# TensorE takes half of a repetition's queries between the first tile's state and the second tile's keys

## The chip, the cores and the metric

The kernel runs on one core of a Trainium2 chip. The metric is the time of one execution on the device in microseconds (us). A core has TensorE (PE; its weight loads are listed apart as PEld), VectorE (DVE), ScalarE (ACT), GpSimd (POOL) and SyncE (SP, which here only issues DMAs). They run side by side and wait for each other on semaphores.

## The reference

One transformer layer over 4 sequences of 2048 tokens with 256 features. The first half is a linear attention with 16 heads of 16 features, the second a mixture of eight experts of which each token takes two:

```
q = relu(x Wq + bq);  k = relu(x Wk + bk);  v = x Wv + bv
q_ = [q*sin(place), q*cos(place)];  k_ = [k*sin(place), k*cos(place)]
kv = k_^T v                        (one state for each head of a sequence)
attn = (q_ kv) / max(q_ . sum(k_), 1e-4)
x = layernorm(x + attn Wo + bo)
gate = softmax of the 2 largest of x router_w^T
out = sum over the 2 experts e of gate_e * (gelu(x w1_e^T) w2_e^T)
x = layernorm(x + out)
```

The state of a sequence needs all of its 2048 tokens before the first of them can be attended to.

## The kernel before

The 8192 tokens are cut into 32 pairs of two tiles of 128 tokens. A repetition of the first stage (`rep`, 0 to 31) projects pair `i = rep` to keys, values and queries, and from repetition `LAG` = 9 on also attends pair `j = rep - 9`, which belongs to the sequence before. Repetitions 10 to 31 project the attention of pair j-1 out, and 11 to 31 also route pair j-2 to its experts. Then 135 expert steps follow, which also finish the attention of the last pairs. Products are made of three float32r passes (`PASSES`: high x high, high x low, low x high), so a product over 256 features is six matmuls.

The order of the work is written out by hand: each engine has its own function `step(u, rep)`, and waits on semaphores that the others raise. Repetitions 0 to 3, 8 to 11, 16 to 19, 24 to 27, 30 and 31 are straight code on TensorE, those between run as loops of two repetitions (`pipeline`). The numbers of the waits are then worked out in registers.

TensorE's order in a repetition from 9 on is: `keys_values` of tile 0 (L540, waits for the low part of x), `attend` of tile 0 (L577, waits for the query's low part L1185 and, from repetition 12 on, for L1171 of VectorE), `state` of the second tile of the pair before (L560), `keys_values` of tile 1 (its wait `k_ready` is for ACT's last read of the first tile's keys and values, L851), `attend` of tile 1, `project_out` of pair j-1 (L629, L631), `rank` (L641 to L645), `state` of tile 0 of this pair, `queries` of both halves (L613, twelve matmuls of 256 columns into the two halves of one PSUM bank), and `attention_transposed` (L600, four transposes). The last one waits for the division of the attention rows by their denominators (`at_ready`, L1058) and for `la_read`, the sum at L1091, in which VectorE reads the banks that `project_out` wrote and that the transposes write next.

```
                if rep > 0:
                    pe.wait_ge(q32_ready, i)
```

is how `queries` waits for ACT to have read the queries of the repetition before (the ReLU at L913). With its second half it raises `q_done`.

ACT's order: key ReLU, router part and the two scaled copies of the values for tile 0 (L847 to L851), cosine part of tile 0 (L831), high part of the next x (L823), the normalised rows of pair j-2 (L860; waits until earlier rows in the same buffer have been scattered), cosine part of tile 1 (L831), high part of a query (L877), an exponential (L881), keys and values of tile 1 (L847 to L851), the copy of the transposes (L869), the ReLU of the queries (L913, waits for `q_done`).

VectorE's order: sine part of tile 0 (L1047), after a whole sequence the state (L1068 on), the choice of experts (L1108 to L1125), sine part of tile 1 (L1047), the division (L1054 to L1058), the residual (L1150), the sum (L1091), the low part of a query (L1185), gates (L1132 to L1141), statistics (L1155, L1156), positions (L1171, L1175), means and logits, and the low part of the transposes (L1179). POOL makes the low part of x (L1576) and scatters the finished rows to the experts' regions in HBM (L1586): two scatters, then, behind the division of the current pair, two more.

Of the kernel before, what the change touches and what calls it, by code (L numbers as in the profile page):

```python
# [44 lines left out]
LAG = PB + 1  # L45
# [63 lines left out]
def build(nc, x, xT, WqT, bq, WkT, bk, WvT, bv, WoT, Wo, bo, bo_columns, rwT, w1T, w2T, consts, out):  # L109
# [4 lines left out]
    with ctx:  # L114
# [257 lines left out]
        def parts(rep):  # L372


            return (LAG <= rep, LAG < rep, LAG + 1 < rep, rep % PB == 0 and PB <= rep, PB <= rep)

        def lagged(u, rep):

            slot = (rep - LAG) % 2
            return u * 2 + (rep % 2 - LAG), u + (rep % 2 - LAG - slot) // 2  # L380
# [145 lines left out]
        def _(pe):  # L526
# [3 lines left out]
            def keys_values(i, rep, h):  # L530
                t = i * 2 + h
                if h == 0 and rep < XLO_POOL:
                    pe.wait_ge(xlo_ready, i + 1)
                elif h == 0:
                    pe.wait_ge(xlo_late, i - (XLO_POOL - 1))
                if rep > 0 or h > 0:
                    pe.wait_ge(k_ready, t)
                def product(n, bank, weights, columns):
                    k, (a, b) = n // len(PASSES), PASSES[n % len(PASSES)]
                    return nc.tensor.matmul(PS[:, bank, 0:columns], xs[:, rep % 2, a, k, h * P:(h + 1) * P], weights[:, b, k, :],  # L540
                                            start=(n == 0), stop=(n == 3 * KD - 1 and bank == bV), skip_group_check=True)

                for n in range(3 * KD):
                    product(n, bK, wk, KE)
                if rep == 0 and h == 0:
                    pe.wait_ge(bias_step, BIAS)
                nc.tensor.matmul(PS[:, bK, 0:D], ones_r[:], bias_k[:], start=False, stop=True, skip_group_check=True)  # L547
                for n in range(3 * KD):
                    mm = product(n, bV, wv, D)
                mm.then_inc(kv_done, 1)  # L550

            def state(t, rep_t):
                pe.wait_ge(k_ready, t + 1)
                pe.wait_ge(ones_ready, t + 1)
                if rep_t % NT_B == 0 and rep_t > 0:
                    pe.wait_ge(state_step, STATE * (rep_t // NT_B - 1) + STATE_READ)
                for half in range(KD):
                    for g in range(NQ):
                        rows_g = slice(g * QUAD, (g + 1) * QUAD)
                        mm = nc.tensor.matmul(PS[rows_g, bST, half * SW:(half + 1) * SW], kr[:, rep_t % 2, half, rows_g],  # L560
                                              vs[:, rep_t % 2, half, :, g, :],
                                              start=(rep_t % NT_B == 0 and half == 0), stop=(rep_t % NT_B == NT_B - 1),
                                              skip_group_check=True)
                mm.then_inc(st_done, 1)

            def attend(j, rep, h, ranked=None):
                if h == 0:
                    pe.wait_ge(qlo_ready, j + 1)
                    if ranked is not None:
                        pe.wait_ge(pos_step, ranked * POS + POS_READ)  # L570
                    if (rep - LAG) % PB == 0:
                        pe.wait_ge(state_step, STATE * ((rep - LAG) // PB + 1))
                if rep > LAG or h > 0:
                    pe.wait_ge(o_done, j * 2 + h)
                for half in range(KD):
                    for n, (a, b) in enumerate(PASSES):
                        mm = nc.tensor.matmul(PS[:, bN + half, 0:2 * NW], qs[:, a, half, h * P:(h + 1) * P],  # L577
                                              sts[:, b, half].rearrange("p a b -> p (a b)"),
                                              start=(n == 0), stop=(n == 2))
                mm.then_inc(n_done, 1)  # L580

            def router_products():
                pe.wait_ge(s_won, 16)
                pe.wait_ge(rw_step, 1)
                for m in range(KD):
                    for k in range(KD):
                        nc.tensor.matmul(PS[:, bA, m * E:(m + 1) * E], won[:, k, m * P:(m + 1) * P], rw[:, k, 0, :],
                                         start=(k == 0), stop=(k == KD - 1))
                for k in range(KD):
                    mm = nc.tensor.matmul(PS[:, bA, KD * E:(KD + 2) * E], ones_r[:].bitcast(F32),  # L590
                                          rw[:, k].rearrange("p a e -> p (a e)"), start=(k == 0), stop=(k == KD - 1))
                mm.then_inc(rw_done, 1)
# [11 lines left out]
            def queries(i, rep, halves):  # L604
                if rep > 0:
                    pe.wait_ge(q32_ready, i)
                if rep == 0:
                    pe.wait_ge(proj_low, 4)
                for half in halves:
                    n = 0  # L610
                    for k in range(KD):
                        for a, b in PASSES:
                            mm = nc.tensor.matmul(PS[:, bQ, half * PAIR:(half + 1) * PAIR],  # L613
                                                  wq[:, a, k, half * P:(half + 1) * P], xs[:, rep % 2, b, k, :],
                                                  start=(n == 0), stop=(n == 3 * KD - 1))
                            n += 1
                if KD - 1 in halves:
                    mm.then_inc(q_done, 1)

            def project_out(j, rep):  # L620
                pe.wait_ge(thi_ready, j + 1)
                if rep == LAG:
                    pe.wait_ge(proj_low, 6)
                    pe.wait_ge(bias_step, BIAS_OUT)
                for h, bank in ((1, bC), (0, bA)):
                    for n, (a, b, k) in enumerate(HIGH_FIRST):
                        if h == 1 and n == 2 * KD:
                            pe.wait_ge(tlo_ready, j + 1)
                        nc.tensor.matmul(PS[:, bank, 0:KE], aT[:, a, k, h * P:(h + 1) * P], wo[:, b, k, :],  # L629
                                         start=(n == 0), stop=False)  # L630
                    mm = nc.tensor.matmul(PS[:, bank, 0:KE], ones_r[:], bias_o[:], start=False, stop=True)  # L631
                mm.then_inc(w_done, 1)
# [15 lines left out]
            def step(u, rep):  # L648
                attn, onward, route, _, _ = parts(rep)
                i = u * 2 + rep % 2  # L650
                j = lagged(u, rep)[0]
                last = rep == NPAIR - 1
                if rep == LAG:
                    pe.wait_ge(dve_const, 2)
                    pe.wait_ge(pool_const, POOL_CONST)
                keys_values(i, rep, 0)
                if attn:
                    attend(j, rep, 0, j - 3 if rep > LAG + 2 else None)
                if 1 <= rep:
                    state(i * 2 - 1, 2 * rep - 1)  # L660
                if rep < LAG:
                    queries(i, rep, (0,))
                keys_values(i, rep, 1)
                if last:
                    queries(i, rep, (0, 1))
                if attn:
                    attend(j, rep, 1)
                if last:
                    pe.wait_ge(table_step, 1)
                if onward:  # L670
                    project_out(j - 1, rep - 1)
                if route:
                    rank(j - 2, rep - 1, j)
                state(i * 2, 2 * rep)
                if not last:
                    queries(i, rep, (1,) if rep < LAG else (0, 1))
                if rep == PRODUCTS_REP:
                    router_products()
                if last:
                    pe.wait_ge(k_ready, 2 * NPAIR)  # L680
                    table_turned(FIRST_MADE, bK)
                    state(i * 2 + 1, 2 * rep + 1)
                if attn:
                    attention_transposed(j, rep)
                if rep == NPAIR - 2:
                    counted(EARLY_PAIRS, EARLY_PAIRS + 1)
# [7 lines left out]
            def table_turned(n, bank):  # L694
                pe.wait_ge(table_step, n)
                nc.tensor.matmul(PS[0:2, bank, P:2 * P], table[:], ident, start=True, stop=True)\
                    .then_inc(tbl_done, 1)

            pipeline(pe, step)


# [70 lines left out]
            for s in range(STEPS):  # L772
# [20 lines left out]
                rep = None if j is None else LAG + j  # L793
# [965 lines left out]
```

## Time and profile before

| | us |
|---|---|
| median of 3 runs | 858.84 |
| lowest and highest of them | 858.13, 859.87 |
| the profiled execution | 858.07 |
| its span, first to last instruction | 856.3 |
| TensorE busy, of the span | 800.6 |
| VectorE busy | 566.9 |
| ACT busy | 460.2 |
| POOL busy | 428.8 |

Every number of the rows below comes from the one profiled execution, whose time is 1.8 us above its span. The first stage ends about 315 us into the span, the expert steps take the rest. A timeline row gives the start in us from the span's start, the duration in us, engine, line, operation, what is written and read, and how many instructions were merged; in brackets stands how long the engine was idle before, and what ended the wait. Matmuls overlap, so durations of neighbouring rows overlap too, and distances between starts are the safer measure.

### The profile page before, as it was taken

How to read it: one execution, taken by the hardware profiler on the slowest of the kernel's cores; microseconds unless marked ns; L12 is line 12 of the kernel's file. 1: busy time of each engine (PE TensorE's matmuls, PEld its weight loads, DVE VectorE, ACT ScalarE, POOL GpSimd, SP SyncE). 2: the span in 40 equal slices, each digit the busy share in tenths (PEclk: the TensorE clock that was granted, in tenths of full speed). 3: DMA queues.
4: the chain of work that ended last, by engine and by line, in shares of the span. 5: the costliest groups of instructions: out<-in, count | busy, mean ns of one | idle time of the engine just before them, and what ended most of it. 6: DMA issues, size and time to landing. Idle time of an engine off the chain costs nothing.

```text
span 856.3 us, 22053 instructions
## 1 busy us (share of the span) xinstructions
PE 800.6 (93%) x6684; PEld 736.7 (86%) x6684; DVE 566.9 (66%) x1816; ACT 460.2 (54%) x1044; POOL 428.8 (50%) x545
## 2 busy tenths in 40 slices
PE   5999999999899869999999999999999999999990
PEld 4888999889899858999899999989999999999980
DVE  3336788878888766666766666664444477777773
ACT  3556676666766644445444544434444445566653
POOL 3886566666677663444445444553222234444442
PEclk9999999999999978999999999999999999999996
DMA  6444033333333242332333332232322355666644
GB/s 195 164 139 133 26 115 121 101 102 107 105 101 101 89 154 82 101 96 89 90 102 106 101 98 85 88 107 82 120 76 78 122 186 191 223 224 215 227 168 172
DMA packets 56469, 106.64 MB, mean 125 GB/s; under 512 B 9262, under 2 KB 37552, under 8 KB 54449
## 3 DMA queue, kind: packets, MB, share of 16 engines
q1 hardware_dynamic: 41296, 63.25, 25.0%
q0 software_dynamic: 12624, 33.84, 10.8%
q10 hardware_dynamic: 2448, 8.26, 2.6%
q8 instruction: 58, 0.95, 0.5%
q14 instruction: 43, 0.34, 0.1%
HBM read 61.91 MB, written 44.32 MB: 124 GB/s over the span
## 4 chain that ended last, share of the span: by engine, by line
PE 80%; DVE 6%; issue 5%; ACT 5%; DMA 3%; SPq 1%; POOL 1%; ACTq 0%; POOLq 0%; DVEq 0%
PE PS L736 23%; PE PS L724 22%; PE PS L540 10%; PE PS L754 7%; PE PS L577 4%; PE PS L713 4%; PE PS L613 4%; PE PS L629 3%; PE PS L600 1%; PE PS L560 1%; ACT vs L851 1%; DMA boc<-in_bo_columns 1%; ACT vs L850 1%; PE PS L547 1%; DVE o L1047 1%
## 5 line engine op out<-in xcount | busy, mean ns | idle before, releaser
L1670 POOL DMA_INDIRECT token_rows<-xg x135 | 134.8, 998 | 284.0 <-DVE xg L1403 261.6
L736 PEld LDWEIGHTS PS<-w,hT 128*128 128x128 f32 x1620 | 211.7, 189 | 13.5 <-issue 3.7
L724 PE MATMUL PS<-w,xgT 128*128 x810 | 222.9, 411 | 0.0
L736 PE MATMUL PS<-w,hT 128*128 x1620 | 218.3, 284 | 0.8 <-ACT hT L994 0.8
L724 PEld LDWEIGHTS PS<-w,xgT 128*128 128x128 f32 x810 | 143.8, 191 | 24.3
L1586 POOL DMA_INDIRECT expert_rows<-rows,idx x128 | 131.0, 1024 | 60.1 <-issue 35.4
L994 ACT ACTIVATE hT<-PS 128x512 fp32r<-128x512 f32 x135 | 80.7, 598 | 142.1 <-PE PS L754 138.4
L990 ACT ACTIVATE hg<-PS 128x512 f32<-128x512 f32 x135 | 80.5, 596 | 118.4 <-PE PS L724 106.4
L1468 DVE TENSOR_TENSOR hT<-PS,hT 128x512 fp32r<-128x512 f32 x135 | 93.4, 692 | 75.6 <-ACT hT L994 75.6
L1395 DVE TENSOR_TENSOR xgT<-PS,xgT 128x256 fp32r<-128x256 f32 x135 | 57.0, 422 | 75.6 <-ACT xgT L960 57.6
L754 PE MATMUL PS<-cst,hg 128*128 128x128 f32 x540 | 81.5, 273 | 0.7 <-ACT hg L990 0.7
L540 PE MATMUL PS<-wk,xs 128*128 128x264 f32 x384 | 65.0, 306 | 15.0 <-DVE wv L1333 8.3
L1403 DVE SCALAR_TENSOR_TENSOR xg<-PS,xg 128x256 f32<-128x256 f32 x135 | 65.2, 483 | 19.1 <-PE PS L736 8.5
L540 PEld LDWEIGHTS PS<-wk,xs 128*128 128x128 f32 x384 | 52.0, 194 | 22.3 <-ACT vs L851 12.5
L577 PE MATMUL PS<-sts,qs 128*128 128x272 f32 x384 | 61.9, 298 | 8.2 <-DVE oh L1171 3.2
L754 PEld LDWEIGHTS PS<-cst,hg 128*128 128x128 f32 x540 | 62.8, 141 | 1.4 <-ACT hg L990 1.4
L577 PEld LDWEIGHTS PS<-sts,qs 128*128 128x128 f32 x384 | 52.3, 192 | 9.8 <-issue 6.5
L613 PE MATMUL PS<-xs,wq 128*128 128x256 f32 x384 | 57.9, 297 | 0.0
L629 PE MATMUL PS<-wo,aT 128*128 128x264 f32 x384 | 57.5, 289 | 0.0
L540 PE MATMUL PS<-wv,xs 128*128 128x256 f32 x384 | 57.0, 285 | 0.0
L713 PE MATMUL PS<-cst,xg 128*128 128x128 f32 x270 | 52.6, 277 | 4.3 <-DMA xg<-expert_rows 4.2
L860 ACT ACTIVATE rows<-xtok,shift,rstd 128x512 f32<-128x512 f32 x64 | 48.8, 818 | 8.9 <-DMA expert_rows<-rows,idx 6.3
(179 smaller groups left out, 1276.5 us busy)
## 6 DMA issues: line engine op xcount, KB each, us to landing
xg<-expert_rows SPq DMA_DIRECT2D x135, 130.0 KB
z<-token_rows SPq DMA_DIRECT2D x15, 1024.0 KB
xraw<-in_xT SPq DMA_DIRECT2D x32, 256.0 KB
xtok<-in_x SPq DMA_DIRECT2D x32, 256.0 KB
out_y<-z ACTq DMA_DIRECT2D x15, 512.0 KB, 3.2
wraw<-in_w1T SPq DMA_DIRECT2D x7, 512.0 KB, 3.8
wraw<-in_w2T SPq DMA_DIRECT2D x7, 512.0 KB, 3.6
token_rows<-xg POOLq DMA_INDIRECT x135
```

What stands on the lines that cost most here:

```text
L540: return nc.tensor.matmul(PS[:, bank, 0:columns], xs[:, rep % 2, a, k, h * P:(h + 1) * P], weights[:, b, k, :], start=(n == 0), stop=(n == ...
L577: mm = nc.tensor.matmul(PS[:, bN + half, 0:2 * NW], qs[:, a, half, h * P:(h + 1) * P], sts[:, b, half].rearrange("p a b -> p (a b)"), star ...
L613: mm = nc.tensor.matmul(PS[:, bQ, half * PAIR:(half + 1) * PAIR], wq[:, a, k, half * P:(half + 1) * P], xs[:, rep % 2, b, k, :], start=(n ...
L629: nc.tensor.matmul(PS[:, bank, 0:KE], aT[:, a, k, h * P:(h + 1) * P], wo[:, b, k, :], start=(n == 0), stop=False)
L713: mm = nc.tensor.transpose(PS[:, gX, k * P:(k + 1) * P], xg[:, XG_SLOTS[s % NXG], k * P:(k + 1) * P], ident)
L724: mm = nc.tensor.matmul(PS[:, gH, :], xgT[:, s % 2, a, k, :], w[:, bass.ds(e, 1), b, k * F:(k + 1) * F].rearrange("p o f -> p (o f)"), sta ...
L736: return nc.tensor.matmul(PS[:, gY, 0:D], hT[:, a, k, :], w[:, bass.ds(e, 1), b, HALF + k * D:HALF + (k + 1) * D] .rearrange("p o f -> p ( ...
L754: mm = nc.tensor.transpose(PS[:, gT, k * P:(k + 1) * P], hg[:, k * P:(k + 1) * P], ident)
L994: nc.scalar.activation(hT[:, 0].rearrange("p k t -> p (k t)"), PS[:, gT, :], ACT.Copy)\
L1468: nc.vector.tensor_tensor(hT[:, 1].rearrange("p k t -> p (k t)"), PS[:, gT, :], hT[:, 0].rearrange("p k t -> p (k t)").bitcast(F32), ALU.s ...
L1586: nc.gpsimd.indirect_dma_start(ex, bass.IndirectOffsetOnAxis(ap=idx[:, slot, h, k:k + 1], axis=0), rows[:, slot, h, k, :], None).then_inc( ...
L1670: nc.gpsimd.indirect_dma_start(yd, bass.IndirectOffsetOnAxis(ap=xg[:, XG_SLOTS[s % NXG], C_DST:C_GATE].bitcast(U32), axis=0), xg[:, XG_SLO ...
```

## The change

In repetitions 9 to 30 the first half of the queries (six matmuls) is issued between the state and the second tile's keys, as repetitions 0 to 8 already do it; the second half stays where both were. Repetition 31 is as before. `LAG` is 9, `last` is repetition 31.

```diff
@@ -658,7 +658,7 @@
                     attend(j, rep, 0, j - 3 if rep > LAG + 2 else None)
                 if 1 <= rep:
                     state(i * 2 - 1, 2 * rep - 1)
-                if rep < LAG:
+                if not last:
                     queries(i, rep, (0,))
                 keys_values(i, rep, 1)
                 if last:
@@ -673,7 +673,7 @@
                     rank(j - 2, rep - 1, j)
                 state(i * 2, 2 * rep)
                 if not last:
-                    queries(i, rep, (1,) if rep < LAG else (0, 1))
+                    queries(i, rep, (1,))
                 if rep == PRODUCTS_REP:
                     router_products()
                 if last:
```

## Rows read from the trace of the kernel before

**Rows 1.** The page: busy us, share of the span, instructions
```profile
PE 800.6 (93%) x6684; PEld 736.7 (86%) x6684; DVE 566.9 (66%) x1816; ACT 460.2 (54%) x1044; POOL 428.8 (50%) x545
```

**Rows 2.** Waits: who waited for whom, us in total, times, longest
```profile
PE PS L540 <- ACT vs L851: 5.9, 18, 2.1
...
PE PS L600 <- DVE lsum L1091: 0.5, 2, 0.4
...
ACT rows L860 <- DMA expert_rows<-rows,idx: 6.3, 5, 2.0
```

**Rows 3.** Timeline of PE, repetition 27 and the start of 28
```profile
253.22 0.97 PE L540 MATMUL PS<-wk,xs 128*128 128x264 f32 x6
...
254.85 0.91 PE L577 MATMUL PS<-sts,qs 128*128 128x272 f32 x6
255.69 0.44 PE L560 MATMUL PS<-vs,kr 128*32 128x66 f32 x16
256.29 1.00 PE L540 MATMUL PS<-wk,xs 128*128 128x264 f32 x6 [0.15 <-ACT vs L851]
...
257.95 0.91 PE L577 MATMUL PS<-sts,qs 128*128 128x272 f32 x6
...
261.03 1.71 PE L613 MATMUL PS<-xs,wq 128*128 128x256 f32 x12
262.57 0.60 PE L600 MATMUL PS<-cst,o 128*128 128x128 f32 x4
262.93 0.49 PE L540 MATMUL PS<-wk,xs 128*128 128x264 f32 x2
```

**Rows 4.** Timeline of PE, repetition 25
```profile
235.59 0.99 PE L577 MATMUL PS<-sts,qs 128*128 128x272 f32 x6 [1.61 <-DVE oh L1171]
236.51 0.44 PE L560 MATMUL PS<-vs,kr 128*32 128x66 f32 x16
236.88 1.00 PE L540 MATMUL PS<-wk,xs 128*128 128x264 f32 x6
...
243.16 0.60 PE L600 MATMUL PS<-cst,o 128*128 128x128 f32 x4
```

**Rows 5.** Timeline of DVE, repetition 27
```profile
254.10 0.17 DVE L1171 TENSOR_TENSOR oh<-oh,PS 128x32 f32<-128x32 f32 x1
...
261.77 0.17 DVE L1091 TENSOR_TENSOR lsum<-PS,lx 128x16 f32<-128x16 f32 x1
```

**Rows 6.** Timeline of DVE, repetition 11
```profile
100.01 0.17 DVE L1091 TENSOR_TENSOR lsum<-PS,lx 128x16 f32<-128x16 f32 x1
```

**Rows 7.** Timeline of PE, repetition 11
```profile
100.32 0.63 PE L600 MATMUL PS<-cst,o 128*128 128x128 f32 x4 [0.19 <-DVE lsum L1091]
```

**Rows 8.** Timeline of ACT, repetition 27
```profile
253.99 0.83 ACT L913 ACTIVATE q<-PS,bqc 128x256 f32<-128x256 f32 x2
```

**Rows 9.** Timeline of PE, repetition 22, and one row of 23
```profile
204.47 0.44 PE L560 MATMUL PS<-vs,kr 128*32 128x66 f32 x16
205.27 1.00 PE L540 MATMUL PS<-wk,xs 128*128 128x264 f32 x6 [0.36 <-ACT vs L851]
...
211.56 0.63 PE L600 MATMUL PS<-cst,o 128*128 128x128 f32 x4
...
215.40 1.00 PE L540 MATMUL PS<-wk,xs 128*128 128x264 f32 x6 [0.36 <-ACT vs L851]
```

**Rows 10.** Timeline of DVE, repetition 22
```profile
211.25 0.17 DVE L1091 TENSOR_TENSOR lsum<-PS,lx 128x16 f32<-128x16 f32 x1
```

**Rows 11.** Timeline of DVE, repetition 25
```profile
242.36 0.16 DVE L1091 TENSOR_TENSOR lsum<-PS,lx 128x16 f32<-128x16 f32 x1
```

**Rows 12.** Timeline of PE, repetition 9
```profile
80.66 0.66 PE L600 MATMUL PS<-cst,o 128*128 128x128 f32 x4 [0.45 <-DVE o L1058]
```

**Rows 13.** Timeline of ACT, repetition 28
```profile
267.39 1.52 ACT L860 ACTIVATE rows<-xtok,shift,rstd 128x512 f32<-128x512 f32 x2 [0.54 <-DMA expert_rows<-rows,idx]
268.82 0.46 ACT L831 ACTIVATE tcos<-PS,cst 128x272 f32<-128x272 f32 x1
```

## Prediction

> Repetitions are counted from 0; the change touches 9 to 30, 22 of them. K, A, S, P, Q, T stand for TensorE's steps in one of them: K keys (with values), A attention, S state, P output projection, Q queries, T the transposes of the attention rows; 0 and 1 behind them are the first and second tile.
>
> **What bounds the kernel now.** I read the page first: TensorE is busy for 93% of the span [rows 1]. So its order of work is the thing to look at, and time can only be gained in its gaps. Then the waits of TensorE [rows 2]: the one this edit aims at is K1 waiting for ACT's scaled values of the first tile (L851), 18 times, 5.9 us in all. The wait of T for the logits' sum on VectorE (L1091) is small, 0.5 us in two places, but it shows that T stands right behind a VectorE chain. Then the timeline of an ordinary repetition, 27: K0 starts at 253.22 and the next K0 at 262.93, a period of 9.71 [rows 3]. S starts at 255.69 and K1 at 256.29, 0.60 later, where an unstalled S takes 0.37 [rows 4]; so about 0.2 us are lost there. A1 starts at 257.95, T at 262.57: 4.62 us of unbroken TensorE work, of which Q is 1.54 (261.03 to 262.57).
>
> Beside those 4.62 us runs a chain that starts with A1: ACT's cosine part (L831), and on VectorE the sine part (L1047), the division (L1054 to L1058), the residual (L1150) and the sum at L1091, which ends at 261.94 (261.77 + 0.17) [rows 5]. T waits for the division and for that sum. The sum is 0.63 us ahead of T here. How close T can follow is seen in repetition 11, where T waited for it: the sum ended at 100.18 and T began at 100.32, 0.14 behind [rows 6 and 7]. So T is free to move up by 0.63 - 0.14 = 0.49 us and no further.
>
> **The change part by part.** Six matmuls of Q (half of 1.54, 0.77 us) go from just ahead of T to between S and K1, in each of the 22 repetitions. Nothing else is added but a second wait for the queries' ReLU of the repetition before (L913), which is long over at that point (it ends at 254.82 [rows 8], and the queries would start at 256.06): I cost it at nothing; if the loop's register work for it were exposed, some 0.04 us each, 0.9 in all. No DMA and no other engine's order changes; the ReLU still waits for the second half, and it comes behind T's copy on ACT in any case.
>
> At K1: S + 0.77 is 1.14 us instead of 0.60. The stall is gone (values were ready at 0.60), but K1 and with it A1 start 0.54 later. That is the flaw: 0.77 us of work is put into a hole of 0.2.
>
> At T: TensorE has only 4.62 - 0.77 = 3.85 us of work from A1, the VectorE chain needs 3.99 (257.95 to 261.94) plus 0.14. So T follows the chain: 4.13 instead of 4.62, 0.49 saved. Net so far +0.05.
>
> A second cost comes in at A0. It waits for a VectorE step (L1171) that stands behind the sum in VectorE's order: it ended 1.05 us after K0 (254.27), K0 being 0.99 after the sum, so 2.04 after it. When T and the next K0 follow the sum at 0.14 and 0.50, this step ends 1.54 after K0 and A0, which began 1.63 after it, has to wait until 1.68 (0.14 behind it): +0.05. An A0 that has waited is also longer to S: 0.92 (235.59 to 236.51) against 0.84 (254.85 to 255.69) [rows 3, 4]. Other repetitions show up to 0.95, so I take +0.10; without it the sum below loses about 0.7 us.
>
> The Trainium skill, TensorE: Matmul & The Clock Gate, section LDWEIGHTS, puts a weight load at columns / 1.2 in ns, 107 ns for 128 columns, and its Part 2 has PE pull loads ahead of running matmuls; one behind a stall has nothing to hide under. By that rule this term is 0.11 in place of 0.10, and the trace agrees (0.08 more) [rows 3, 4]; were no load exposed, the sum below would be 5.8 instead of 6.5.
>
> Ordinary repetition: A1 +0.54 + 0.05 + 0.10 = +0.69, sum at L1091 at 262.63, T at 262.77 instead of 262.57: **+0.20**. Four are of this kind (10, 18, 26, 27): 0.8.
>
> Repetitions 12 to 15 and 20 to 23 run as loops on TensorE and VectorE. There the VectorE chain is longer, so less can be saved at T. Repetition 22: S at 204.47, K1 at 205.27 with a wait of 0.36 [rows 9]; 0.80 becomes 1.14, +0.34. The sum ends at 211.42 [rows 10] and T starts 0.14 behind, at 211.56 already: nothing is saved. **+0.34.** In 11 to 15 and 21 to 23, eight repetitions, S to K1 is 0.59, 0.46, 0.59, 0.72, 0.66, 0.54, 0.80 and 0.79 (the last one ends at 215.40), and the sum ends 0.14 to 0.51 ahead of T. The same working gives 0.25 (repetition 11), 0.31, 0.72, 0.41, 0.34, 0.56, 0.34 and 0.27, together 3.2; the 0.72 is repetition 13, where A0 begins to wait as well.
>
> Batch starts (17, 25) [rows 4]: A0 waits 1.61 us, so ACT is long done and K1 follows S unstalled (236.51 and 236.88). All 0.77 delays A1, 0.50 comes back at T (the sum ends at 242.52, T starts at 243.16: 0.64 less 0.14) [rows 4, 11]. With 0.15 more at A0 that is +0.4 each; the repetitions ahead of them (16, 24), where VectorE's state work (L1063 on) hides K1's delay, come out at 0. Together 0.8.
>
> Repetition 9: T already waits for the division [rows 12], K1 did not wait: the whole **0.77**.
>
> Late scatters (19, 20, 28, 29, 30): ACT waits for the landing of scattered rows before it normalises, five times, 6.3 us [rows 2]. These scatters are issued after the division, which now comes 0.49 later against the next K0 (0.69 less 0.20). The first late repetition of each of the two rows of them takes this on; K1's delay is hidden in the rest. +0.49 at 19, -0.07 at 20, +0.5 over 28 to 30: 0.9.
>
> The Trainium skill's DMA: Bandwidth & Descriptors gives about 2.0 us of fixed cost for a DMA. With that landing, scatters that end 2.2 us after K0 would be in at 4.2, before ACT needs them, and this term would be 0 and the sum 5.6. The trace differs: in repetition 28, where they end 1.7 after K0, ACT was held for 0.54 until 267.39 [rows 13].
>
> Sum: 0.8 + 3.2 + 0.8 + 0.77 + 0.9 = **6.5 us** more in the loop. Behind it, the first expert rows, the count and the tables hang on the same VectorE and POOL chain and shift with it; the 135 expert steps are unchanged. On the profiled execution, 858.07 (span 856.3 and 1.8 around it), that is 864.6. The median of the three runs is 0.8 above that execution; on it, 865.3. I name 865.0, since a little of the 0.10 terms may be hidden.
>
> Bounds: per repetition the change can't cost more than 0.77 (22 times, 16.9 us), nor gain more than the stalls at K1: S to K1 over 0.37 in all 22 is 5.1 us. The unknown parts are whether T's smaller room in loop code stays (0.14 against 0.63, eight times 0.49, 3.9 us) [rows 9, 10] and the scatters (0 to 4 us).
>
> **Rivals.**
> 1. T is not held by VectorE: TensorE simply fills the holes at K1. For it: those waits are real, 5.9 us [rows 2], and T hardly waits now. Against: T's room of 0.63 us in one case, of 0.14 in the other, and an actual wait [rows 3, 5 to 7, 9, 10]. It gives 858.8 - 5.1 = 853.7. It decides as soon as T starts less than 3.9 us behind A1. Chance 7%.
> 2. K1's delay is absorbed: ACT's normalisation, not A1, sets the cosine part, as in the five late repetitions. In repetition 28 normalising starts at 267.39 and the cosine part at 268.82 [rows 13]. If most repetitions looked so, T would hardly move: 858.8, within 1.7. Against: 17 of 22 have ACT waiting for A1. Chance 13%.
> 3. Scatter landings go late in more repetitions, since each is issued later against the next use. The five late ones now take up to 0.8 us over an ordinary 9.71; five or six more of that kind add 4: 869. For it: two of the five came one behind the other, so lateness is carried on. Against: the cycle from division to division is no shorter than before, so its slack is the same. Chance 15%.
> The forecast, T bound by VectorE and K1 pushed back, has 65%, with a range of its own of 861.5 to 868.
>
> **How the numbers follow.** What a measurement of this kernel can tell from no change is about 0.2%, 1.7 us: 857.1 to 860.6. Slower is the forecast and rival 3, 80%; same is rival 2 with the weak end of the forecast, 13%; faster is rival 1, 7%. The range takes in most of rivals 2 and 3: 859.5 to 870.
>
> **What would show it.** In the profile after: no wait of K1 for L851 from repetition 9 on, S to K1 about 1.14; T waiting for L1091 or L1058 in nearly all of the 22, some 0.2 to 0.7 us each, in place of two entries; A0 starting about 1.7 after K0 in repetitions like 27; a period of about 9.9 there and 10.3 in the loops; L860 waiting for the scatters about as often as now. The forecast is wrong if T is seldom held and these periods stay at 9.7 and 10.0.

## The result, and the profile after

The changed kernel takes 862.18 us (median of 7 runs, 860.05 to 862.9) against 858.84 before (over all seven of its runs as well, 856.17 to 859.87): ratio 1.0048, 95% interval [1.0031, 1.0066]. That is slower, by 3.3 us where 6.2 were named. The profiled execution took 860.05, its span 858.2. Its spans can't be subtracted as they stand: the start of repetition 9 is at 69.10 in it and at 71.53 in the execution of before, a difference of the kernel's first part, which the change doesn't touch. From there to the start of repetition 31 it is 223.36 us before and 227.81 after, **+4.45**, and from there to the end 561.36 and 561.32. So in this pair of executions the whole price lies in the 22 repetitions.

The page after (busy us, share, instructions) answers to [rows 1]: TensorE does the same matmuls.

```profile
PE 798.1 (93%) x6684; PEld 733.8 (86%) x6684; DVE 567.3 (66%) x1816; ACT 460.4 (54%) x1044; POOL 432.5 (50%) x545
```

The waits of TensorE and two of other engines, after (who waited for whom, us in total, times, longest), answer to [rows 2]. K1's 18 waits for L851 have no row any more; T's wait for the sum has gone from 2 times to 16, and POOL's scatters wait longer for the division (21.4 us in 12 places before). The view shows no idle time under 0.15 us, so the 16 is too few: by the starts, T follows the sum by 0.14 or 0.15 in every repetition from 10 to 30, before only in 11, 14, 19 and 22.

```profile
PE PS L600 <- DVE lsum L1091: 5.5, 16, 0.7
PE PS L577 <- DVE oh L1171: 3.4, 2, 1.7
...
PE PS L600 <- DVE o L1058: 1.6, 2, 1.2
...
POOL expert_rows L1586 <- DVE o L1058: 38.5, 20, 4.5
```

The timeline of TensorE after, repetition 27, answers to [rows 3]. S to K1 is 1.19 (257.05 to 258.24), of which the six queries are 0.82. A1 to T is 4.13 (259.79 to 263.92), as worked out. The period is 9.78 (254.52 to 264.30) against 9.71.

```profile
254.52 0.98 PE L540 MATMUL PS<-wk,xs 128*128 128x264 f32 x6
...
256.16 0.96 PE L577 MATMUL PS<-sts,qs 128*128 128x272 f32 x6
257.05 0.44 PE L560 MATMUL PS<-vs,kr 128*32 128x66 f32 x16
257.42 0.98 PE L613 MATMUL PS<-xs,wq 128*128 128x256 f32 x6
258.24 0.90 PE L540 MATMUL PS<-wk,xs 128*128 128x264 f32 x6
...
259.79 0.91 PE L577 MATMUL PS<-sts,qs 128*128 128x272 f32 x6
...
262.87 0.99 PE L613 MATMUL PS<-xs,wq 128*128 128x256 f32 x6
263.92 0.63 PE L600 MATMUL PS<-cst,o 128*128 128x128 f32 x4
264.30 0.49 PE L540 MATMUL PS<-wk,xs 128*128 128x264 f32 x2
```

The timeline of VectorE beside it answers to [rows 5]: the sum ends at 263.78, 3.99 behind A1, and T starts 0.14 behind the sum, both as before.

```profile
255.87 0.18 DVE L1171 TENSOR_TENSOR oh<-oh,PS 128x32 f32<-128x32 f32 x1
...
263.61 0.17 DVE L1091 TENSOR_TENSOR lsum<-PS,lx 128x16 f32<-128x16 f32 x1
```

### The profile page after: what moved, and what is told of

Same layout as the page of the kernel before. It is cut to its first block, busy times and chain, and to the rows that moved or that the text cites. A ratio compares the mean times of both kernels' runs of the same rounds, so it can differ in the third digit from the quotient of the medians.

```text
span 858.2 us, 22053 instructions
## 1 busy us (share of the span) xinstructions
PE 798.1 (93%) x6684; PEld 733.8 (86%) x6684; DVE 567.3 (66%) x1816; ACT 460.4 (54%) x1044; POOL 432.5 (50%) x545
## 4 chain that ended last, share of the span: by engine, by line
PE 78%; DVE 9%; issue 4%; DMA 3%; ACT 3%; SPq 1%; POOL 1%; another core or an unknown queue 0%; DVEq 0%; ACTq 0%; POOLq 0%
PE PS L736 22%; PE PS L724 21%; PE PS L540 9%; PE PS L754 7%; PE PS L577 5%; PE PS L613 4%; PE PS L713 3%; PE PS L629 2%; PE PS L600 2%; PE PS L560 1%; DVE o L1047 1%; ACT tcos L831 1%; DMA expert_rows<-rows,idx 1%; DMA xraw<-in_xT 1%; DVE den L1056 1%
## 5 line engine op out<-in xcount | busy, mean ns | idle before, releaser
L1586 POOL DMA_INDIRECT expert_rows<-rows,idx x128 | 133.9, 1046 | 69.0 <-DVE o L1058 38.5
L540 PE MATMUL PS<-wk,xs 128*128 128x264 f32 x384 | 61.8, 297 | 11.1 <-DVE wv L1333 8.5
L540 PEld LDWEIGHTS PS<-wk,xs 128*128 128x128 f32 x384 | 51.2, 191 | 15.1 <-DVE wv L1333 8.5
L613 PE MATMUL PS<-xs,wq 128*128 128x256 f32 x384 | 62.9, 300 | 0.0
L540 PE MATMUL PS<-wv,xs 128*128 128x256 f32 x384 | 56.4, 283 | 0.0
L613 PEld LDWEIGHTS PS<-xs,wq 128*128 128x128 f32 x384 | 50.1, 191 | 5.8
```

The costliest lines, as they stand in the source:

```text
L1586: nc.gpsimd.indirect_dma_start(ex, bass.IndirectOffsetOnAxis(ap=idx[:, slot, h, k:k + 1], axis=0), rows[:, slot, h, k, :], None).then_inc( ...
```

## The experiments

Ratios are to the kernel before, run on the same chip in the same series. There are three such series, e1 to e4, e5 to e8, and e9 and e10, in which the kernel before took 857.51, 855.75 and 853.01; so compare ratios between them, not times. In the timelines of experiments the line numbers of some kernels are 1 to 3 higher.

**e1: the changed kernel again**, no edit.

> The changed kernel once more, for a second profile of it. The loop from the keys of repetition 9 to those of 31 took 223.4 us before and 227.8 in the profile after, +4.4, while the spans differ by only 1.9, since that execution began its repetition 9 2.4 us earlier. Theory (T follows VectorE's sum at L1091, K1 is pushed back): the loop takes 227 to 229 us again, T waits for L1091 in most repetitions, the time is 0.3 to 0.6% over the kernel before, and the start before repetition 9 differs by up to 2 us from execution to execution. Rival (the +4.4 is chance, by where late scatter landings fell): the loop comes out near 224 to 225 in this profile.

Measured: 861.21, ratio 1.0034 [1.0018, 1.0051]. The price stands, 3.7 us (1.5 to 4.4 by the interval), and T again follows the sum by 0.15 everywhere. The expected length of the loop failed: 230.95 us, not 227 to 229. Repetitions 18, 19, 25 and 30 are 0.6 to 1.4 longer than in the first execution. The longest, 25 (13.18 against 11.81), is a stretch at the lower of TensorE's two clock levels: the view by windows gives a granted clock of 0.50 (1.2 GHz) behind the wait of A0 (columns: us, busy us of PE, PEld, DVE, ACT, POOL with instructions, granted clock, DMA share, GB/s).

```profile
236.00:239.40 3.40, 1.69 (x20) 1.37 (x22) 3.16 (x16) 1.65 (x7) 1.41 (x3) 1.00 0.22 78
239.40:242.80 3.40, 3.40 (x30) 3.22 (x25) 2.74 (x14) 2.48 (x4) 3.05 (x4) 0.50 0.00 0
```

In the first profiled execution the same place ran at 1.00, so this is a cost of some executions. It was also seen in e3 (25), e4 (17) and e7 (17), not in the eight other profiles. In 18 and 19 of e1 TensorE ran as before and the chain to the sum was longer (4.80 and 4.62 in place of 3.98), in 18 with ACT held for the landing of scattered rows for 1.73 us.

**e2 and e3: a shorter residual**, in the kernel before and in the changed one. The addition at L1150 is done for 32 of each 256 columns only; the rest of the residual is left out.

```diff
-nc.vector.tensor_tensor(r, PS[:, bA:bC + 1, 0:D], r, ALU.add)
+nc.vector.tensor_tensor(r[:, :, 0:32], PS[:, bA:bC + 1, 0:32], r[:, :, 0:32], ALU.add)
```

> The kernel before, with the residual on VectorE (L1150, 0.68 us) cut to 32 of 256 columns: the other columns of the attention's output aren't added, so part of the computation is left out. It is the base for the next run. Theory: T of the kernel before isn't held by VectorE, so the shorter chain gives nearly nothing, 0 to 1 us less than the kernel before (856 to 859). Rival (VectorE's whole load is what counts): 32 residuals less 0.5 us each would give 10 us or more.

> The changed kernel with the same shortened residual (32 of 256 columns, part of the computation left out). Theory: VectorE's chain from A1 to the sum shrinks by about 0.5 us, from 3.99 to 3.5, under TensorE's 3.85 us of work, so T is no longer held and the holes filled at K1 are kept: 2 to 5 us less than the kernel before with the short residual. In an ordinary repetition the period falls to about 9.45. Rival (moving work ahead of K1 costs as such, by K1 coming later, whatever T does): it stays 3 to 4 us above the kernel before with the short residual.

Measured: e2 852.16, ratio 0.9934 [0.9916, 0.9952]; e3 854.85, ratio 0.9963 [0.9948, 0.9978]. The first expectation failed (5.4 us less, not 0 to 1), though T stands 0.57 us or more behind the sum in each of its repetitions 10 to 30: VectorE's chain counted in the kernel before too, as far as two executions tell by way of the late scatters. In the profiles the loop is 3.0 us shorter, and the late repetitions 19, 20 and 28 to 30 alone are 3.0 shorter; ACT's waits for landings nearly vanish (1.4 us in 3 places, against 6.3 in 5).

The second failed as a total: e3 stays 2.7 us over e2. By repetitions it is mixed, as e3 less e2 in the profiles:

| repetitions | e3 less e2 | after less before |
|---|---|---|
| ordinary: 10, 18, 26, 27 | -0.6 | +0.4 |
| 11 to 15, 21 to 23 | -0.2 | +1.9 |
| 16, 17, 24, 25 | +2.7 | +0.4 |
| 9 | +0.3 | +1.3 |
| 19, 20, 28 to 30 | +1.8 | +0.5 |

So with the shorter chain the six queries ahead of K1 gain in the ordinary repetitions and cost nothing in the loops, which is what T's hold by VectorE predicts. The loss lies in 25 (2.1, most of it the stretch at 1.2 GHz), 17 (0.6, where K1 has no hole in front of it) and the late repetitions. The hold is also not gone, only smaller: in 14 of the 21 repetitions from 10 to 30 T still starts 0.15 or 0.16 behind the sum, because there the chain takes 3.7 to 4.5 us and not 3.5. The plain case is 9.48 in repetition 26. In others a thing shows that I had not counted. The timelines of TensorE, POOL and ACT in e3, repetition 27:

```profile
254.16 0.87 PE L540 MATMUL PS<-wv,xs 128*128 128x256 f32 x6
...
256.08 0.97 PE L612 MATMUL PS<-xs,wq 128*128 128x256 f32 x6
257.08 1.00 PE L540 MATMUL PS<-wk,xs 128*128 128x264 f32 x6
```

```profile
254.33 0.96 POOL L1587 DMA_INDIRECT expert_rows<-rows,idx  x1 [0.30 <-issue]
```

```profile
255.84 0.39 ACT L848 ACTIVATE kr<-PS 128x256 f32<-128x256 f32 x1 [0.99 <-PE PS L540]
```

The values' matmuls end at 255.03 by the record, ACT sees them at 255.84, 0.81 later, half a us after POOL has finished issuing a scatter (255.29). K1, which needs ACT's copies (the last ends at 257.02), comes at 257.08, 1.00 behind the queries' start where it is 0.82 without a wait, so a hole opens behind the six queries too. The same update came on time in the first execution of the changed kernel: the values' matmuls end at 256.33, and ACT starts while POOL is still issuing (255.73 to 256.69).

```profile
256.36 0.38 ACT L847 ACTIVATE kr<-PS 128x256 f32<-128x256 f32 x1 [0.23 <-PE PS L540]
```

That the scatters are what makes it late in e3 is therefore not shown; more on this at the end.

**e4: three matmuls instead of six** between S and K1 (0.4 us into a hole of 0.2), nine ahead of T.

```diff
+            def early(rep):
+                return 3 * KD if rep < LAG else 3
...
+                if not last and early(rep):
+                    queries(i, rep, 0, early(rep))
```

> Only three of the twelve query matmuls go between S and K1 in repetitions 9 to 30 (0.38 us instead of 0.77), the other nine stay. Theory (a hole of 0.2 to 0.4 us is there to be filled, and T has 0.49 us of room in ordinary repetitions and less in loop code): K1 is about where it is in the kernel before (S to K1 0.80 at most, and its first weight load hidden), T comes up to 0.38 us earlier, and the period of an ordinary repetition is about 9.45; 2 to 5 us less than the kernel before (854 to 857). Rival (any queries ahead of K1 cost in proportion): half of the change's loss, 1.5 to 2 us more than the kernel before.

Measured: 856.99, ratio 0.9993 [0.998, 1.0005]: level, so neither the gain of 2 to 5 us nor the rival's loss. The ordinary repetitions came out as worked out (26, 27, 28: 9.46, 9.47, 9.47, against 9.71 before), so the size of the piece decides there. But 12 to 15 gained nothing (39.43 us together against 39.44 before), with T 0.15 behind the sum in each of them, and repetition 17 lost 1.6 to a stretch at a clock of 0.50.

**e5: the same, and in repetitions 9, 17 and 25 the six queries ahead of A0**, where the 1.6 us of waiting are.

```diff
+                if attn and rep % PB == 1:
+                    queries(i, rep, 0, 3 * KD)
                 if attn:
                     attend(j, rep, 0, j - 3 if rep > LAG + 2 else None)
...
+                if not last and early(rep) and not (attn and rep % PB == 1):
+                    queries(i, rep, 0, early(rep))
```

> Three query matmuls between S and K1 as in the run with three, but in repetitions 9, 17 and 25 six of them ahead of A0, where TensorE idles 1.6 to 1.7 us for VectorE's state work. Theory (only holes of the right size gain; VectorE's chain from A1 bounds T): ordinary repetitions 9.47 instead of 9.71, repetitions 17 and 25 about 10.9 instead of 11.33, no idle stretch of 1.6 us and so no stretch at half clock within the loop; 1 to 3 us less than the kernel before. Rival (the run with three was level with before because moving queries ahead of K1 gains nothing at all): level again, within 0.5 us.

Measured: 853.82 (851.16 to 855.55), ratio **0.9973 [0.9957, 0.9989]**: this version is faster than both kernels, by a quarter of a per cent over the one before. Its loop is 2.6 us shorter than before in the profiles: 0.8 in the ordinary repetitions, 0.9 in 16, 17, 24 and 25, 1.0 in the late ones, nothing in the loops. The last of these is not the edit's for sure, since the late ones differ by more between executions of one kernel (1.3 between after and e1). The start of the batch in repetition 25, TensorE: the queries stand in the wait, of which 0.88 is left, and K1 follows S by 0.37.

```profile
230.39 0.98 PE L612 MATMUL PS<-xs,wq 128*128 128x256 f32 x6
232.24 0.98 PE L577 MATMUL PS<-sts,qs 128*128 128x272 f32 x6 [0.88 <-issue]
233.15 0.44 PE L560 MATMUL PS<-vs,kr 128*32 128x66 f32 x16
233.52 1.00 PE L540 MATMUL PS<-wk,xs 128*128 128x264 f32 x6
```

**e6 to e8: scatters 3 and 4 right behind 2**, not behind the division, in before, after and e5.

```diff
                     scatter(1 - slot, 0, 1)
-                    pool.wait_ge(at_ready, j + 1)
-                    hold(pool)
                     scatter(1 - slot, 1, 0)
```

> The kernel before, with POOL's third and fourth scatter of a repetition issued right behind the second instead of behind the current pair's division. Theory on the late semaphores (updates that TensorE gives with L540, L631, L645, L560 arrive up to 1.0 us after the matmul's recorded end when they overlap a POOL scatter issue): POOL's last scatter now ends before the values' matmuls do, so the update of L540 comes on time and S to K1 in repetitions 22 to 24 falls from 0.80 to 0.87 to about 0.6. Scatters land earlier too, so L860 waits in fewer than 5 repetitions: 1 to 4 us less than the kernel before. Rival (the lateness belongs to TensorE's own register work in loops): S to K1 in 22 to 24 stays at 0.8.

> The changed kernel with the same order of scatters. Theory: K1 is set by TensorE's own work, so ordinary repetitions stay at 9.8 and loops at 10.0 to 10.4; the late repetitions go, as in the kernel before with this order; 2 to 5 us more than that one. Rival (the change costs time because it pushes the division and with it the scatters behind it later): its loss against the kernel before with this order falls under 1 us.

> The same order of scatters with three queries ahead of K1 and six ahead of A0 at batch starts. Theory: the two gains add, 2 to 6 us less than the kernel before. Rival (they compete for the same slack): no better than the better one of the two.

Measured: 873.88, 871.36 and 871.93; ratios 1.0218 [1.0194, 1.0242], 1.018 [1.0155, 1.0206] and 1.0194 [1.0171, 1.0218]. ACT waits for no landing any more, and 16 to 18 us are lost all the same, so all three theories failed. Two rivals came true by their numbers, e7 being 2.5 us under e6 and e8 no better than e7, but beside a loss of 16 us that says little about the price of the change. S to K1 in 22 to 24 of e6 is 0.67, 0.67 and 0.59, as its theory had it; but it is 0.67, 0.67 and 0.60 in e9 too, where no scatter was moved, so that decides nothing either. The timelines of PE, POOL and ACT in e6 at the end of a repetition:

```profile
286.26 0.60 PE L600 MATMUL PS<-cst,o 128*128 128x128 f32 x4
286.61 0.72 PE L540 MATMUL PS<-wk,xs 128*128 128x264 f32 x4
288.09 0.41 PE L540 MATMUL PS<-wk,xs 128*128 128x264 f32 x2 [0.75 <-issue]
```

```profile
285.07 0.96 POOL L1586 DMA_INDIRECT expert_rows<-rows,idx  x1 [0.30 <-issue]
286.33 0.96 POOL L1586 DMA_INDIRECT expert_rows<-rows,idx  x1 [0.30 <-issue]
```

```profile
288.42 0.60 ACT L869 ACTIVATE aT<-PS 128x512 fp32r<-128x512 f32 x1 [3.66 <-remote]
```

T ends at 286.86 by the record; ACT copies its result 1.56 later, 1.13 after the last of four scatters (287.29). TensorE itself stands for 0.75 in the middle of K0, with no semaphore of the profile to wait for. In e6 such pauses ahead of matmuls of L540 and L600 add up to 11.8 us in 21 places. So the wait for the division does not only order the buffers: it keeps four issues from standing in a row, and where they do, 16 to 18 us are lost. By what way the issues stop TensorE is not shown.

**e9 and e10: what the batch starts alone are worth.** e9 is the kernel before with the edit of e5 in 9, 17 and 25 and nothing else; e10 is the changed kernel with it, so that it has six matmuls elsewhere where e5 has three.

```diff
e9:  return 3 * KD if rep < LAG else (3 * KD if rep % PB == 1 else 0)
e10: return 3 * KD
```

> The kernel before, but in repetitions 9, 17 and 25 the first half of the queries stands ahead of the first tile's attention, where TensorE waits 1.6 us for L1171 in the last two; nowhere else is a matmul moved. Theory (T follows VectorE's sum, holes are worth filling only where there is one): the 0.77 goes into the hole, S and K1 stay where they are, T moves up by the 0.50 it has over the sum in 17 and 25 and by nothing in 9, where it already waits for the division: 1.0 us less in the loop, ratio about 0.999. Rival (the gain of the version with three matmuls elsewhere, 2.3 us, came from the two batch starts alone): 2 us or more less, ratio at or under 0.9975.

> The changed kernel with the six matmuls ahead of the first tile's attention in repetitions 9, 17 and 25, and between the state and the second tile's keys in all the others. Theory: 17 and 25 lose what the change put on their second tile (11.80 and 11.81 become about 11.0, as in the version with three matmuls elsewhere), 9 loses 0.7 of its 1.25, the other 19 repetitions stay as in the changed kernel: 2.3 us under it, level with the kernel before or 0.15% over it, and some 2.5 us over the version with three matmuls. Rival (six or three matmuls elsewhere make no difference, only the batch starts do): level with that version, ratio about 0.9975.

Measured: e9 853.1, ratio 1.0 [0.9988, 1.0013]; e10 855.92, ratio 1.0039 [1.0023, 1.0055]. e9 is as expected within its interval (its loop is 1.4 us shorter than before), and both rivals fall; but e10 is not level with the kernel before or 0.15% over it, as its theory said, and is 5.6 us over e5 by the ratios, not 2.5. The gain of e5 doesn't come from the batch starts alone, and three or six matmuls elsewhere are not the same (0.9973 against 1.0039, intervals apart, though from two series; 5.4 us between the two loops in the profiles, for 19 repetitions). The batch starts do what was expected, 10.86 and 10.87 for 17 and 25 in e9 (11.34 and 11.33 before), 10.99 and 10.98 in e10, but it is not seen in the median: repetition 18, right behind, takes 10.70 and 10.74 in place of 9.71. Its cause is a landing, first e9 (POOL, ACT), then the execution of before in the same repetition:

```profile
161.18 0.96 POOL L1589 DMA_INDIRECT expert_rows<-rows,idx  x1 [0.30 <-issue]
```

```profile
165.59 1.52 ACT L863 ACTIVATE rows<-xtok,shift,rstd 128x512 f32<-128x512 f32 x2 [1.68 <-DMA expert_rows<-rows,idx]
```

```profile
162.32 0.96 POOL L1586 DMA_INDIRECT expert_rows<-rows,idx  x1 [0.30 <-issue]
```

```profile
165.35 1.54 ACT L860 ACTIVATE rows<-xtok,shift,rstd 128x512 f32<-128x512 f32 x2
```

In e9 the last issue ends at 162.14 and ACT may go on at 165.59, 3.45 later. Before, it ended at 163.28 and ACT did not have to wait at 165.35, so the rows had landed within 2.07. Why one landing takes so much longer than another is left open. It need not be the shorter repetition 17: e1 has the same wait in 18 (10.61, the last issue ends at 164.72 and ACT goes on at 168.20) behind a 17 that is not shortened, and e5 shortens 17 to 10.98 and has 9.53 in 18.

## Why the prediction was right, and where its sizes were off

**K1's hole and T's chain: right.** The wait for L851 goes, K1 comes later, T follows the sum by 0.14, and A1 to T is 4.13: each as worked out. Against rival 1 (TensorE fills the holes) stand T right behind the sum in all 21 repetitions from 10 on, e3 beside e2, where a shorter chain turns the loss of the ordinary repetitions into a gain, and e4 and e10 beside e5: the same matmuls at the same place cost time as six and gain or cost nothing as three. The size was not right: 6.2 us were named for the median, and 3.3 and 3.7 were measured. In ordinary repetitions loss and gain nearly cancel (9.78 against 9.71, where about 9.9 was named), so that small errors in the terms count for much, and that the total lies in the range owes something to the range's width, 859.5 to 870. By periods, in us:

| repetitions | forecast | measured |
|---|---|---|
| ordinary: 10, 18, 26, 27 | 0.8 | 0.4 |
| 11 to 15, 21 to 23 | 3.2 | 1.9 |
| 16, 17, 24, 25 | 0.8 | 0.4 |
| 9 | 0.77 | 1.25 |
| 19, 20, 28 to 30 | 0.9 | 0.5 |
| sum | 6.5 | 4.45 |

**Ordinary, term "+0.69 at A1": it was +0.54.** Three terms were off. A0 hardly waits (1.64 after K0, as before) and is 0.89 to S, not 0.94. The six queries take 0.82, not 0.77. And K1 is shorter behind them. K1 to the first matmul of its values is 0.95 before (257.24 less the 256.29 of [rows 3]) and 0.84 after (259.08 less 258.24). Timeline of PE, first before, then after:

```profile
257.24 0.88 PE L540 MATMUL PS<-wv,xs 128*128 128x256 f32 x6
```

```profile
259.08 0.87 PE L540 MATMUL PS<-wv,xs 128*128 128x256 f32 x6
```

I had charged such an effect at A0, where a wait would appear, and forgotten to pay it back at K1. It does not hang on the wait alone: in 9, 17 and 25 before, K1 followed S without one and was as long. Timeline of PE before, repetition 25, where K1 is at 236.88 [rows 4]:

```profile
237.83 0.87 PE L540 MATMUL PS<-wv,xs 128*128 128x256 f32 x6
```

That is 0.95 again, and behind the six queries it is 0.85 in all 22 repetitions. In e3, repetition 27, where it stands behind the queries and has to wait, it is 0.95 too. So it takes both, the longer matmuls in front (256 columns each, where those of S have 66) and no wait. That they hide K1's first weight load is the likely reason, not shown by itself. The Trainium skill, TensorE: Matmul & The Clock Gate, section LDWEIGHTS, makes such a load 0.107 us by its rule, and these rows agree (0.11); with 0.11 in 22 repetitions 2.4 us come off the sum. This term, put at nothing, is the largest single error.

**Batch starts and the repetitions ahead of them.** 17 and 25 cost 0.46 and 0.48, where 0.4 each was named. 16 and 24, named 0, came out 0.23 and 0.31 shorter.

**Loop repetitions, term "nothing is saved at T" (0.34 in 22): it was 0.03.** Of the difference 0.11 is K1's. For the rest, I took VectorE's longer chain there as its own. It was not. Timeline of VectorE, PE and POOL before, repetition 22:

```profile
209.76 0.69 DVE L1058 TENSOR_TENSOR o<-o,den 128x512 f32<-128x512 f32 x1
210.64 0.69 DVE L1150 TENSOR_TENSOR xtok<-PS,xtok 128x512 f32<-128x512 f32 x1 [0.18 <-PE PS L631]
```

```profile
209.25 0.28 PE L631 MATMUL PS<-bias_o,ones_r 128*128 128x264 f32 x1
```

```profile
209.10 0.96 POOL L1586 DMA_INDIRECT expert_rows<-rows,idx  x1 [0.30 <-issue]
```

The residual could have followed the division at once. It waited for a matmul that by the record had ended at 209.53, 1.11 earlier, while POOL was issuing a scatter until 210.06. After, the same step starts right behind the division:

```profile
210.95 0.69 DVE L1058 TENSOR_TENSOR o<-o,den 128x512 f32<-128x512 f32 x1
211.56 0.68 DVE L1150 TENSOR_TENSOR xtok<-PS,xtok 128x512 f32<-128x512 f32 x1
```

A1 to the end of the sum falls from 4.48 (206.94 to 211.42) to 4.21 (208.12 to 212.33), and T moves up by that 0.27. The row of L1150, right above the one in [rows 10], names the wait; I had taken the chain's length without it. How long the chain is in the loops is also not the change's alone: in e9, which does the same work in the same order there as the kernel before, A1 to the sum is 4.21 in 22 too, and the period 9.80. Against e9 the change costs 2.4 us in these eight repetitions, against before 1.9. The working of their 3.2 does not come out whole either: by the rule of the text repetition 11 gives 0.54 and not 0.25, 13 gives 0.58 and not 0.72, and the eight 3.3.

**Repetition 9, 0.77: it was 1.25.** The 0.77 came nearly whole (0.7). The other 0.55 lies ahead of it: A0 starts 3.37 after K0, not 2.82, behind the state's low part. VectorE, before and after:

```profile
72.76 1.44 DVE L1087 TENSOR_TENSOR sts<-st,sts 128x544 fp32r<-128x544 f32 x1
```

```profile
71.19 1.13 DVE L1087 TENSOR_TENSOR sts<-st,sts 128x544 fp32r<-128x544 f32 x1
```

It ends 2.67 and 3.22 after its K0. Here POOL still splits weights, and VectorE's passes of this size take 0.86 to 1.44 us where 0.69 is usual. How the two fall against each other differs from execution to execution: e2, whose TensorE does the same as before there, had 10.08 against 9.55, and e1, the changed kernel again, 10.44 against 10.80. So this part is not the change's.

**Late scatters, 0.9 us: chance.** It was 0.5 in one execution of the changed kernel and 1.8 in the other, without that one's repetition 18. Two executions of the same changed kernel had their late repetitions at 20 and 28 to 30, and at 18 to 20 and 28 to 30. That rival 3 did not come true is as forecast (6 waits for landings against 5, in both executions, of 7.6 and 10.4 us against 6.3).

**Rival 2** (delay absorbed) holds at most in 14, 16, 19, 24 and 30, which are level or shorter, not in the ordinary ones.

The loop's +4.45 is the difference of two single executions, and e1's loop is 7.6 over that of before; the medians differ by 3.3 and 3.7 us. What is left between these is within what executions of one kernel differ by (856.2 to 859.9 before; what follows the loop takes 561.3 in before and after and 558.9 in e1).

## What to carry to other kernels

A piece of work that is moved into a hole must not be larger than the hole, and what it leaves must not already be followed closely by another engine: measure both rooms in every kind of repetition, and cut the piece to the smaller (three matmuls here, six where the wait is 1.6 us). When a step starts long after its input by the record ended, look at what the other engines were doing before you book its length as work. Where transfers are only just in time, look at the repetition behind a shortened one as well: a late landing there took back the gain twice (e9, e10), though it is not shown that the one brought the other.

## What was not expected of the hardware

The semaphore updates of TensorE can reach other engines late: by 0.8 us to ACT in e3, by 1.1 to the residual in the kernel before, by 1.56 behind T in e6. In repetitions without scatters (9 to 11) the same updates are within 0.04 us of the recorded end. The Trainium skill, Perfetto Trace Analysis, section Tensor Engine Instruction (MATMUL, LD_WEIGHTS), says that the end of a matmul in a profile is estimated and that the update goes out only when PSUM has acknowledged the write, so such a gap does not show in the row itself.

POOL's indirect DMA issues (L1586, 0.96 us and more) have to do with it, but are not enough. Over the twelve profiles, from 70 to 300 us and without the copies of the transposes that the view puts down to an older matmul, 675 waits ended with TensorE, and 60 of them more than 0.2 us after the recorded end. All 60 had an issue that ended between 0.5 us before and 0.7 us after that end; of the 321 waits without one, none was late. But 294 waits with such an issue were on time as well, and in after, e1, e9 and e10 not one was late. What tells the late ones from the others is open. Moving the issues (e6 to e8) didn't settle it: it made the kernel 16 to 18 us slower and left late updates in each of the three.

An execution in which TensorE waited some 1.7 us at a batch start may run a stretch of 3.4 us right behind it at 1.2 GHz (e1, 1.4 us lost), and another of the same kernel may not. It was so in four of the eight profiles that have this wait whole (1.1 to 1.7 us), and in none of the four (e5, e8, e9, e10) where six queries stand in it.
